# Four conv layers on one core: layer 1's first rows and stack made during layer 0's last filters, the last image's norm on two engines, and the spectral mixing by one matmul per mode

## Chip, cores, metric

The kernel runs on one core of a Trainium2 chip. The metric is the device time of one execution in microseconds (us). Engines are called PE (TensorE), DVE (VectorE), ACT (ScalarE), POOL (GpSimd) and SP (SyncE, which here only issues DMAs). Each engine works through its own instructions in program order and waits on semaphores.

## What is computed

The input x is (8, 32, 128, 128) in f32. Four residual layers follow, each on the group norm of x (32 groups of one channel):

```python
x = x + L0(_gn(x))   # 3x3 conv, batch norm over all images, relu, then a 5x5 and a 3x3 circular filter per channel
x = x + L1(_gn(x))   # n = sqrt(sum_c of 9 shifted squares); op = tanh(n @ op_w.T + op_b), 9x9 for each pixel;
                     # out = W * (patches + patches @ op)
x = x + L2(_gn(x))   # attention from a blurred, Sobel-filtered channel mean
x = x + L3(_gn(x))   # global transform (16 x 16 Fourier modes, top and bottom) times a 3x3 conv
# L3: top = einsum('bixy,ioxy->boxy', c_ft[:, :, :16, :16], w1r + 1j * w1i), bot likewise with w2
```

In L3, each of 32 x 16 kept modes multiplies a complex vector of 32 input channels by its own complex 32 x 32 matrix, for 8 images.

## The kernel before

**Layer 0's filters** (about 300 to 757 us) go image by image (h = 0 to 7), eight turns n of four channels each. A turn is filter5 (L632) and filter3 (L639) on PE, `gradient` on ACT (L957, squares the 3x3 result), `curvature` on DVE (L1423, L1426, and the statistics L1230). Woven into the turns of image h is the finish of image h-1: PE sums its statistics (`group_means`, `group_vars`), DVE makes scale and shift, ACT normalises 32 channels (L938) at turns 1 and 2 and squares them (L964) at 3 and 4, DVE sums the squares over the channels (`channel_sums`, L1435) at 4 and 5, ACT takes the root at 6 (L1021), and DVE splits it into three bf16 parts at 7 (`norm_parts`). With h = 8 the loop runs once more, for the finish of image 7 alone.

SP's part for one finished image, in this order: store x1 (L429), store the normalised image with its borders to `pad1` (L431, "pad"), load a later image, then `shifted_norms`: store the three parts (L369), wait for them to land, and issue 18 copies that lay out shifted rows in `rows_dram` (L376).

**Layer 1** (826 to about 3110 us) has 64 chunks (8 images x 8). A chunk needs the stack (12 DMAs from pad1, `stack_in`, L385), rows of norms (`norms_in`, L393), and operator values that are made once and spread out: `operator_rows` on PE (L661, into PSUM banks 6 and 7 for the first two chunks), tanh on ACT (`rows_tanh_out`, L973), a diagonal added (L979) and a cast (L982) in `rows_high`, a remainder (`rows_rest`, L1458 on DVE for the first two chunks, L1170 on POOL later), `rows_middle` (L987), `rows_low` (L1463 or L1175). Then SP stores them (`split_out`, L399), waits for the landing and issues 24 loads (`split_in`, L410). The tile of the rows is single, so tanh of chunk 1 waits until the store of chunk 0 has landed. The steady work of a chunk is 28 multiplies on DVE (L1498), 14 tanh on ACT (L1041) and 14 multiplies on POOL (L1187), mixed by PE (L703).

Between the layers, with h = 8, SP waits for the rows of image 0 and loads three chunks of norms and the stack; PE makes the operator rows of chunks 0 and 1 between `group_means` and `group_vars` of image 7. ACT's queue holds, in this order: normalise, squares, tanh and rows of both chunks, the root, and then, behind a wait for the landing of image 7's pad store (`xn1_stored[1]`), layer 1's first tanh.

**Layers 2 and 3** go image by image. At the end `mix_spectrum` (L869) mixes the modes: for each of 32 x 16 modes one matmul of 32 x 32 weights with the real part and one with the imaginary part of the weights, 1,024 in all; the f32 matmul stands as two in the trace, so 2,048 records. The four quarters of the partitions (rows of the array) write four different banks at any time. ACT copies the result (L1131), SP stores it and loads it back transposed. PE then makes the last image's conv (`conv3`, L591), ACT takes it out (L1082), and the output loop of 8 images begins (ACT L1139 and L1144, PE L889 and L900, DVE L1584 and L1586), fed by loads of x3 (L504) and l3 (L311).

## Time and profile before

| what | us |
|---|---|
| median of 3 runs | 3891.71 (3881.45 to 3893.06) |
| profiled execution, its own time | 3892.53 |
| its span, first to last instruction | 3890.4 |
| busy PE, DVE, POOL, ACT | 3348.1, 2864.0, 2340.5, 1848.2 |
| last turn of layer 0's filters ends | 757 |
| first multiply of layer 1 on POOL | 826.4 |
| image 7 normalised on ACT | 782.6 to 795.0 |
| mixing of modes | 3609.7 to 3688.3 |

In the page, a row has the start, the length in us, the engine, the line, the operation, the tiles and the count. Many f32 tiles have one name, `arena`, so operations are told apart by their line. A matmul's record is longer than the interval to the next one, since they overlap.

### The profile page before, as it was taken

The numbers are of one execution on the slowest core, as the hardware profiler recorded it, in microseconds if no ns is written. First come the engines' busy times: TensorE is split into PE (matmuls) and PEld (weight loads), VectorE is DVE, ScalarE is ACT, GpSimd is POOL, SyncE is SP. The second block draws the span as 40 slices with busy tenths as digits, with TensorE's granted clock in tenths as the row PEclk, the third lists the DMA queues.
The fourth block names the chain that finished last, engine by engine and source line by source line (L and its number), as shares of the span: only waits on it lengthen the run. The fifth ranks groups of instructions, "written<-read, shape, count | busy, mean of one in ns | idle before, by whom it ended". The sixth has DMA issues, their size and how long they took to land.

```text
span 3890.4 us, 89862 instructions
## 1 busy us (share of the span) xinstructions
PE 3348.1 (86%) x32900; PEld 1193.3 (31%) x32900; DVE 2864.0 (74%) x3513; ACT 1848.2 (48%) x2702; POOL 2340.5 (60%) x1131
## 2 busy tenths in 40 slices
PE   4678999749999999999999999999999957888575
PEld 2343444302212222222222212222222236655454
DVE  3652554459989989989989989989999966666034
ACT  0114566355555555555545545545555546666011
POOL 0000000039999999999999999999999952231000
PEclk9899999969999999999999999999999977889565
DMA  6565897576666656656656656656666654645589
GB/s 158 121 160 108 157 197 169 118 176 151 146 141 154 147 137 154 149 135 154 153 132 159 150 130 159 151 129 157 153 145 145 151 149 123 173 122 132 141 193 253
DMA packets 495205, 586.47 MB, mean 151 GB/s; under 512 B 71971, under 2 KB 334755, under 8 KB 489436
## 3 DMA queue, kind: packets, MB, share of 16 engines
q1 hardware_dynamic: 484212, 563.65, 62.7%
q10 hardware_dynamic: 10560, 16.93, 1.8%
q8 instruction: 287, 4.70, 0.5%
q14 instruction: 146, 1.19, 0.1%
HBM read 409.91 MB, written 184.54 MB: 153 GB/s over the span
## 4 chain that ended last, share of the span: by engine, by line
POOL 30%; PE 29%; issue 28%; DVE 5%; ACT 4%; DMA 2%; SPq 1%; ACTq 0%; POOLq 0%; DVEq 0%
POOL arena L1187 27%; PE ps L632 7%; PE ps L591 7%; PE ps L639 4%; PE ps L703 3%; ACT arena L938 2%; PE ps L789 2%; POOL arena L1175 2%; PE ps L685 1%; DVE arena L1546 1%; PE ps L900 1%; PE ps L869 1%; DMA arena<-x_dram 1%; DMA w_conv<-in_conv_w 1%; DVE arena L1584 1%
## 5 line engine op out<-in xcount | busy, mean ns | idle before, releaser
L1187 POOL TENSOR_TENSOR arena<-arena 128x1024 f32<-128x1024 f32 x896 | 1931.1, 2196 | 555.8 <-ACT arena L1041 555.6
L1498 DVE TENSOR_TENSOR arena<-ps,arena 128x1024 f32<-128x1024 f32 x1792 | 2107.0, 1219 | 206.2 <-PE ps L685 173.9
L703 PE MATMUL ps<-arena,w_mix 128*32 128x512 f32 x10752 | 1439.1, 607 | 79.2 <-POOL arena L1187 79.2
L1041 ACT ACTIVATE arena<-ps 128x1024 f32<-128x1024 f32 x896 | 918.1, 1025 | 1028.2 <-PE ps L695 1017.1
L685 PE MATMUL ps<-arena,sel 48*128 48x512 bf16 x3584 | 703.1, 386 | 25.2 <-issue 15.3
L685 PEld LDWEIGHTS ps<-arena,sel 48*128 48x128 bf16 x3584 | 190.2, 93 | 946.3 <-issue 937.9
L591 PE MATMUL ps<-arena,w_conv 32*32 32x512 f32 x9216 | 357.7, 658 | 46.6 <-issue 38.5
L695 PE MATMUL ps<-norms,opw 57*128 57x512 bf16 x1792 | 348.7, 385 | 49.0 <-ACT arena L973 17.5
L703 PEld LDWEIGHTS ps<-arena,w_mix 128*32 128x32 f32 x10752 | 215.0, 108 | 467.6 <-issue 467.6
L938 ACT ACTIVATE arena<-arena,nmr,rstd 128x128 f32<-128x128 f32 x768 | 299.7, 482 | 31.9 <-DVE nmr L1257 31.9
L632 PE MATMUL ps<-arena,circ 128*128 128x512 f32 x640 | 287.9, 595 | 14.3 <-ACT arena L952 14.3
L591 PEld LDWEIGHTS ps<-arena,w_conv 32*32 32x32 f32 x9216 | 182.5, 108 | 186.4 <-issue 129.1
L695 PEld LDWEIGHTS ps<-norms,opw 57*128 57x128 bf16 x1792 | 101.7, 93 | 435.0 <-issue 429.5
L1219 POOL COPY arena<-arena 32x130 f32<-32x130 f32 x32 | 29.2, 913 | 293.9 <-DVE arena L1548 292.9
L1170 POOL TENSOR_TENSOR arena<-arena 128x1024 f32<-128x1024 f32 x62 | 132.9, 2144 | 96.6 <-ACT arena L982 96.6
L1584 DVE TENSOR_TENSOR arena<-arena,ps 128x512 f32<-128x512 f32 x64 | 43.6, 682 | 195.2 <-PE ps L900 166.3
L639 PE MATMUL ps<-arena,circ 128*128 128x512 f32 x384 | 176.3, 594 | 0.0
L632 PEld LDWEIGHTS ps<-arena,circ 128*128 128x128 f32 x640 | 120.4, 189 | 166.8 <-issue 166.8
L1230 DVE BATCH_NORM_STATS2 st<-arena 128x6 f32<-128x128 f32 x768 | 156.5, 276 | 7.0 <-POOL arena L1206 4.9
L1163 POOL TENSOR_TENSOR col<-col,powers 128x1 f32<-128x1 f32 x8 | 4.4, 550 | 244.0 <-DVE col L1286 244.0
L1426 DVE TENSOR_TENSOR arena<-arena 128x512 f32<-128x512 f32 x64 | 44.3, 692 | 143.1 <-ACT arena L957 141.1
L1175 POOL TENSOR_TENSOR arena<-arena 128x1024 bf16<-128x1024 f32 x62 | 133.0, 2145 | 0.0
(151 smaller groups left out, 2165.2 us busy)
## 6 DMA issues: line engine op xcount, KB each, us to landing
arena<-pad SPq DMA_DIRECT2D x768, 260.0 KB, 7.6
split_dram<-arena SPq DMA_DIRECT2D x64, 768.0 KB, 3.6
arena<-split_dram SPq DMA_DIRECT2D x1536, 32.0 KB, 3.1
x_dram<-arena SPq DMA_DIRECT2D x16, 2048.0 KB, 7.4
l_dram<-arena SPq DMA_DIRECT2D x128, 256.0 KB, 4.3
arena<-l_dram SPq DMA_DIRECT2D x32, 1024.0 KB, 14.0
arena<-x_dram SPq DMA_DIRECT2D x16, 2048.0 KB, 15.8
pad<-arena SPq DMA_DIRECT2D x8, 2080.0 KB, 16.2
```

The lines of the kernel that those rows point to most:

```text
L591: m = pe.matmul(ps[C * j:C * j + C, bank + g, :], weights[C * g:C * g + C, dy, dx, :], tile[C * g:C * g + C, r:r + CR, dx:dx + W], start=t ...
L632: m = pe.matmul(ps[:, n % 2, :], circ[:, d, :], yp[h % 2][:, 4 * n:4 * n + 4, 4 - d:4 - d + W], start=d == 0, stop=d == 4)
L639: m = pe.matmul(ps[:, 2 + n % 2, :], circ[:, 5 + d, :], yp[h % 2][:, 4 * n:4 * n + 4, 4 - d:4 - d + W], start=d == 0, stop=d == 2)
L685: m = pe.matmul(ps[:, 2 * (n % 2) + e, :], sel[ROWS2 * e:ROWS2 * e + SPLIT_ROWS, u % GROUP, :], split[ROWS2 * e:ROWS2 * e + SPLIT_ROWS, pa ...
L695: m = pe.matmul(ps[:, POOL_BANK + e, :], opw[ROWS2 * e:ROWS2 * e + KROWS, SPREAD[c], :], norms[ROWS2 * e:ROWS2 * e + KROWS, buf, half, :]. ...
L703: m = pe.matmul(ps[C * g:C * g + C, SUM + chunk % 2, :], w_mix[:, s, :], ring[:, (first + g // 2) % size, NPX * (g % 2):NPX * (g % 2) + NP ...
L938: m = nc.scalar.activation(tile[:, c, :], src[:, c, :], ACT.Identity, scale=rstd[:, gn.slot + n % 2, c:c + 1], bias=nmr[:, gn.slot + n % 2 ...
L1041: nc.scalar.activation(ring_p[:, slot, :], ps[:, POOL_BANK:POOL_BANK + 2, :].rearrange("p a n -> p (a n)"), ACT.Tanh).then_inc(tanh_p, 1)
L1175: nc.gpsimd.tensor_tensor(hml[:, 2, :], rest, hml[:, 1, :], ALU.subtract).then_inc(rows_l, 1)
L1187: nc.gpsimd.tensor_tensor(slot, slot, pixels(chunk % 2, SPREAD[n // 2], n % 2), ALU.mult).then_inc(prod_p, 1)
L1230: m = nc.vector.bn_stats(st[:, c, :], tile[:, c, :])
L1498: nc.vector.tensor_tensor(slot, weights, pixels(par, ONCE[n // 2], n % 2), ALU.mult).then_inc(prod_d, 1)
```

## The change

It has three parts.

- **Transition.** PE makes the operator rows of chunks 0 and 1 at turns 2 and 5 of image 7's filters, ACT and DVE do their share at turns 3 to 7 (the last cast of chunk 1 at turn 0 behind it). SP loads the norms of chunks 0 to 2 already at image 2. It issues `split_out`, 24 `split_in` and the first stack in the turn of image 7, ahead of `shifted_norms` of image 6. `group_vars` of image 7 follows directly on `group_means`.
- **Last image's norm.** ACT normalises channels 0 to 15 and DVE 16 to 31 (`half_norm`). The squares go by 32 columns of all channels, so that each of DVE's channel sums needs one of them only.
- **Mixing.** The weights of a mode lie as 64 columns (real, imaginary), and one matmul makes both products: 512 matmuls in four groups. Rows 0 to 31 and 32 to 63 now write one bank, rows 64 to 95 and 96 to 127 another. Each group is then put together by four ACT copies (the imaginary products, to the own partitions) and eight DVE operations. The mixing uses all eight banks: it waits for the conv before it to be taken out, and the last conv waits for the putting together. The negated copy of the spectrum (one of three L1075) is gone.

Left out of the diff are semaphore names and counts (`dftw_copy` in threes becomes twos; layer 0's batch-norm uses gn0's semaphores in place of two of its own, with the same waits).

```diff
@@ -187,7 +187,8 @@
...
         dog = sb("dog", [P, W + 2])
-        cs = sb("cs", [P, 3, 2, 4, MODES, B])
+        cs = sb("cs", [P, 2, 2, 4, MODES, B])
+        crossed = sb("crossed", [P, 2, NPX])
         ps = ctx.enter_context(nc.psum_tensor("ps", [P, 8, NPX], F32))
@@ -229,7 +230,7 @@
...
-        wm = part(8192, 4 * C * 64).rearrange("p (r t o m) -> p r t o m", r=2, t=2, o=C)
+        wm = part(8192, 4 * C * 64).rearrange("p (t k m) -> p t k m", t=2, k=2 * C)
         ys = part(37512, 2048).rearrange("p (a b m) -> p a b m", a=8, b=B)
@@ -413,15 +415,6 @@
...
                     rows_in(yt[h % 2], image(y_dram, h + 2), yt_loaded[h % 2])
-                if h == B:
-                    sp.wait_ge(c3_mm, 8 * (B - 1))
-                    sp.wait_ge(xn1_stored[0], 16 * (B // 2))
-                    sp.wait_ge(border_done, 16 * BORDERS)
-                    sp.wait_ge(rows_stored[0], 16 * 18 * (B // 2))
-                    norms_in(0, 0)
-                    stack_in(0, 0)
-                    norms_in(0, 1)
-                    norms_in(0, 2)
                 if h == 0:
@@ -432,10 +425,19 @@
...
                     rows_in(xt[par], image(x, h + 1), xt_loaded[par])
-                if h == B:
+                if h == 2:
+                    sp.wait_ge(rows_stored[0], 16 * 18)
+                    for chunk in range(3):
+                        norms_in(0, chunk)
+                if h == B - 1:
                     split_out(0)
...
                     split_in(0, 1)
+                    sp.wait_ge(c3_mm, 8 * (B - 1))
+                    sp.wait_ge(norm_sq, 4 * (B - 1))
+                    sp.wait_ge(xn1_stored[0], 16 * (B // 2))
+                    sp.wait_ge(border_done, 16 * BORDERS)
+                    stack_in(0, 0)
                 shifted_norms(h - 1)
@@ -463,7 +465,8 @@
...
                     if n + 3 == CHUNKS:
-                        sp.wait_ge(rows_stored[1], 16 * 18 * (B // 2))
+                        for par in range(2):
+                            sp.wait_ge(rows_stored[par], 16 * 18 * (B // 2))
                     norms_in((n + 3) // CHUNKS, (n + 3) % CHUNKS)
@@ -538,8 +541,8 @@
...
-            sp.wait_ge(spec_copy, 8)
             for t in range(2):
+                sp.wait_ge(spec_copy, 2 * t + 2)
                 for q in range(4):
@@ -639,14 +642,6 @@
...
-            for h in range(B):
-                for n in range(8):
-                    filter5(h, n)
-                    if n == 1 and h:
-                        group_vars(gn1, h - 1)
-                    filter3(h, n)
-                    if n == 0 and h:
-                        group_means(gn1, h - 1)
             def chunk_after(b, chunk, n):
@@ -663,13 +658,23 @@
...
+            for h in range(B):
+                for n in range(8):
+                    filter5(h, n)
+                    if n == 1 and h:
+                        group_vars(gn1, h - 1)
+                    filter3(h, n)
+                    if n == 0 and h:
+                        group_means(gn1, h - 1)
+                    if n == 2 and h == B - 1:
+                        pe.wait_ge(op_copied, 32)
+                        pe.wait_ge(par_loaded, 16 * PARS)
+                        operator_rows(0, 0, SUM)
+                    if n == 5 and h == B - 1:
+                        pe.wait_ge(rows_tanh, START + 1)
+                        operator_rows(0, 1, SUM)
             group_means(gn1, B - 1)
-            pe.wait_ge(op_copied, 32)
-            pe.wait_ge(par_loaded, 16 * PARS)
-            operator_rows(0, 0, SUM)
             group_vars(gn1, B - 1)
-            pe.wait_ge(rows_tanh, START + 1)
-            operator_rows(0, 1, SUM)
             pe.wait_ge(gn1.shifted, B)
@@ -859,20 +864,21 @@
...
-                for turn in range(4):
+                for grp in range(4):
                     for m_ in range(KX):
+                        x8, ky = 2 * grp + m_ // MODES, m_ % MODES
+                        t, xx = divmod(x8, 4)
                         for q in range(4):
-                            grp = (turn + q) % 4
-                            x8, ky = 2 * grp + m_ // MODES, m_ % MODES
-                            t, xx = divmod(x8, 4)
-                            for r in range(2):
-                                m = pe.matmul(ps[C * q:C * q + C, 4 + grp, 16 * m_:16 * m_ + 16], wm[C * q:C * q + C, r, t, :, xx * MODES + ky],
-                                              cs[C * q:C * q + C, 1 - r:3 - r, t, xx, ky, :], start=r == 0, stop=r == 1)
-                m.then_inc(spec_mm, 1)
+                            rows, at = slice(C * q, C * q + C), 2 * C * (q % 2)
+                            m = pe.matmul(ps[at:at + 2 * C, 4 * (q // 2) + grp, 16 * m_:16 * m_ + 16], wm[rows, t, :, xx * MODES + ky],
+                                          cs[rows, :, t, xx, ky, :], start=True, stop=True)
+                    m.then_inc(spec_mm, 1)
             pe.wait_ge(wm_loaded, 16 * 16)
-            pe.wait_ge(dftw_copy, 3 * B)
+            pe.wait_ge(dftw_copy, 2 * B)
+            pe.wait_ge(conv3_evac, 2 * (B - 1))
             mix_spectrum()
+            pe.wait_ge(spec_copy, 4)
             for half in range(HALVES):
@@ -963,6 +969,14 @@
...
+            def squares_by_columns(h, q):
+
+                if q == 0:
+                    act.wait_ge(norm_sum, 4 * h)
+                    act.wait_ge(gn1.out, 4 * (h + 1))
+                cols = slice(QC * 4 * q, QC * 4 * q + QC * 4)
+                nc.scalar.activation(sqr[:, :, cols], xn1[h % 2][:, :, 1 + cols.start:1 + cols.stop], ACT.Square).then_inc(norm_sq, 1)
+
             def rows_tanh_out(b, chunk, bank):
@@ -1001,19 +1015,23 @@
...
                         for q in (2 * n - 2, 2 * n - 1):
-                            normalise(gn1, h - 1, q, xn1[(h - 1) % 2][:, :, 1:W + 1], xt[(h - 1) % 2])
+                            if h < B or q < 2:
+                                normalise(gn1, h - 1, q, xn1[(h - 1) % 2][:, :, 1:W + 1], xt[(h - 1) % 2])
                     if n in (3, 4) and h:
                         for q in (2 * n - 6, 2 * n - 5):
-                            squares(h - 1, q)
-                    if n == 3 and h == B:
-                        act.wait_ge(c3_mm, 8 * B)
+                            if h < B:
+                                squares(h - 1, q)
+                            else:
+                                squares_by_columns(h - 1, q)
+                    if n == 3 and h == B - 1:
                         rows_tanh_out(0, 0, SUM)
                         rows_high(0, 0)
-                    if n == 4 and h == B:
+                    if n == 4 and h == B - 1:
                         rows_middle(0, 0)
+                    if n == 6 and h == B - 1:
                         rows_tanh_out(0, 1, SUM)
                         rows_high(0, 1)
-                    if n == 5 and h == B:
+                    if n == 7 and h == B - 1:
                         rows_middle(0, 1)
@@ -1071,9 +1089,9 @@
...
                 sp_ = ps[:, 4, 256:256 + 8 * 2 * MODES].rearrange("p (x r y) -> p r x y", x=8, r=2)
-                for n, (r, sign) in enumerate(((1, -1.0), (0, 1.0), (1, 1.0))):
-                    nc.scalar.activation(cs[:, n, :, :, :, t:t + 1].rearrange("p t x y b -> p (t x) (y b)"),
-                                         sp_[:, r, :, :], ACT.Copy, scale=sign).then_inc(dftw_copy, 1)
+                for r in range(2):
+                    nc.scalar.activation(cs[:, r, :, :, :, t:t + 1].rearrange("p t x y b -> p (t x) (y b)"),
+                                         sp_[:, r, :, :], ACT.Copy).then_inc(dftw_copy, 1)
@@ -1125,15 +1143,16 @@
...
-            act.wait_ge(spec_mm, 1)
-            for n in range(8):
-                src = ps[:, 4 + n // 2, 256 * (n % 2):256 * (n % 2) + 256].rearrange("p (y r b) -> p b r y", y=MODES, r=2)
-                nc.scalar.copy(ys[:, n, :, :].rearrange("p b (r y) -> p b r y", r=2), src).then_inc(spec_copy, 1)
-
+            for grp in range(4):
+                act.wait_ge(spec_mm, grp + 1)
+                after(act, spec_copy, grp - 1)
+                for q in range(4):
+                    at = 2 * C * (q % 2) + C
+                    m = nc.scalar.copy(crossed[C * q:C * q + C, grp % 2, :], ps[at:at + C, 4 * (q // 2) + grp, :])
+                m.then_inc(spec_cross, 1)
             for half in range(HALVES):
...
             act.wait_ge(spec_loaded, 16)
-            act.wait_ge(spec_copy, 8)
             with act.Fori(0, B) as b:
@@ -1429,9 +1448,19 @@
...
+            def half_norm(h):
+
+                dve.wait_ge(gn1.ready, h + 1)
+                dve.wait_ge(xn1_stored[h % 2], 16 * (h // 2))
+                for q in (2, 3):
+                    for c in range(QC * q, QC * q + QC):
+                        m = nc.vector.tensor_scalar(xn1[h % 2][:, c, 1:W + 1], xt[h % 2][:, c, :], rstd[:, gn1.slot + h % 2, c:c + 1],
+                                                    nmr[:, gn1.slot + h % 2, c:c + 1], ALU.mult, ALU.add)
+                    m.then_inc(gn1.out, 1)
+
             def channel_sums(h, q):
-                dve.wait_ge(norm_sq, 4 * h + 4)
+                dve.wait_ge(norm_sq, 4 * h + (4 if h < B - 1 else q + 1))
                 nc.vector.tensor_reduce(r2[:, 32 * q:32 * q + 32], sqr[:, :, 32 * q:32 * q + 32].rearrange("p c w -> p w c"),
@@ -1469,17 +1498,20 @@
...
                         group_scale(gn1, h - 1, t)
+                        if h == B:
+                            half_norm(B - 1)
                     if h < B:
...
                             channel_sums(h - 1, q)
-                    if n == 4 and h == B:
+                    if n == 4 and h == B - 1:
                         rows_rest(0, 0)
-                    if n == 5 and h == B:
+                    if n == 5 and h == B - 1:
                         rows_low(0, 0)
-                    if n == 6 and h == B:
+                    if n == 7 and h == B - 1:
                         rows_rest(0, 1)
+                    if n == 0 and h == B:
                         rows_low(0, 1)
@@ -1569,6 +1601,17 @@
...
                     group_scale(gn2, i + 2, t)
+
+            for grp in range(4):
+                dve.wait_ge(spec_cross, grp + 1)
+                for q in range(4):
+                    at = 2 * C * (q % 2)
+                    real, imag = (tile.rearrange("p (x y r b) -> p r x b y", x=2, r=2, b=B)
+                                  for tile in (ps[at:at + C, 4 * (q // 2) + grp, :], crossed[C * q:C * q + C, grp % 2, :]))
+                    own = ys[C * q:C * q + C, 2 * grp:2 * grp + 2, :, :]
+                    nc.vector.tensor_tensor(own[:, :, :, 0:MODES], real[:, 0], imag[:, 1], ALU.subtract)
+                    m = nc.vector.tensor_tensor(own[:, :, :, MODES:KX], real[:, 1], imag[:, 0], ALU.add)
+                m.then_inc(spec_copy, 1)
```

## Rows read from the trace of the kernel before

**Rows 1.** Windows: us, busy per engine (x), clock, DMA share, GB/s.

```profile
1150.00:3250.00 2100.00, 1938.96 (x14797) 464.07 (x14796) 1884.07 (x1734) 1097.59 (x1238) 1928.67 (x902) 0.98 0.63 146
```

**Rows 2.** Timeline of SP's DMA issues between layer 0 and layer 1.

```profile
761.19 11.36 SPq L376 DMA_DIRECT2D rows_dram<-parts_dram  x18
...
776.14 5.89 SPq L385 DMA_DIRECT2D arena<-pad  x12
...
785.22 0.47 SPq L429 DMA_DIRECT2D x_dram<-arena  x1
794.99 0.38 SPq L431 DMA_DIRECT2D pad<-arena  x1
813.05 0.36 SPq L399 DMA_DIRECT2D split_dram<-arena  x1
816.53 11.06 SPq L410 DMA_DIRECT2D arena<-split_dram  x24
...
827.63 0.42 SPq L369 DMA_DIRECT2D parts_dram<-rp  x1
```

**Rows 3.** Timeline of the other engines there; in brackets the idle time before.

```profile
779.32 1.04 PE L661 MATMUL ps<-norms,opu 57*32 57x512 bf16 x8 [20.94 <-DMA norms<-rows_dram]
...
798.16 1.02 ACT L973 ACTIVATE arena<-ps 128x1024 f32<-128x1024 f32 x1
...
807.11 1.22 DVE L1458 TENSOR_TENSOR arena<-arena 128x1024 f32<-128x1024 f32 x1
...
825.33 1.02 ACT L1041 ACTIVATE arena<-ps 128x1024 f32<-128x1024 f32 x1
826.43 8.58 POOL L1187 TENSOR_TENSOR arena<-arena 128x1024 f32<-128x1024 f32 x4 [528.18 <-ACT arena L1041]
...
871.67 3.49 DVE L1498 TENSOR_TENSOR arena<-ps,arena 128x1024 f32<-128x1024 f32 x3 [4.62 <-DMA arena<-pad]
```

**Rows 4.** Timeline of DVE and ACT in image 7's filters.

```profile
743.83 3.68 DVE L1435 TENSOR_REDUCE r<-arena 128x32 f32<-128x1024 f32 x2
...
755.46 0.60 ACT L957 ACTIVATE arena<-ps 128x512 f32<-128x512 f32 x1 [6.09 <-PE ps L639]
```

**Rows 5.** The chain that ended last, in order of time.

```profile
781.58 12.01 DMA arena<-pad
```

**Rows 6.** Line L429 (x1 store), and the landing times of its DMAs.

```profile
L429 SPq DMA_DIRECT2D x_dram<-arena x8: 468/4720/5405, 370.5 to 785.2; - x8
...
DMA to landing us min/median/max: 6.8/15.0/15.6
```

**Rows 7.** DMA issues, 740 to 850 us: size, us to landing.

```profile
pad<-arena SPq DMA_DIRECT2D x1, 2080.0 KB, 15.8
```

**Rows 8.** Windows: one in the gap between the layers.

```profile
775.00:785.00 10.00, 2.03 (x12) 1.09 (x12) 0.74 (x3) 2.68 (x8) 0.00 (x0) 0.50 0.87 186
```

**Rows 9.** Timeline of the mixing of modes and what follows.

```profile
3610.67 2.12 ACT L1082 ACTIVATE arena<-ps,bias 128x1024 f32<-128x1024 f32 x2 [9.24 <-PE ps L591]
3613.37 2.05 PE L869 MATMUL ps<-cs,arena 32*32 32x16 f32 x128 [1.70 <-issue]
...
3621.50 2.05 PE L869 MATMUL ps<-cs,arena 32*32 32x16 f32 x128 [6.08 <-issue]
...
3688.15 11.65 PE L591 MATMUL ps<-arena,w_conv 32*32 32x512 f32 x280
3688.38 2.31 ACT L1131 COPY arena<-ps 128x256 f32<-128x256 f32 x8 [75.59 <-PE ps L869]
...
3723.56 3.50 PE L900 MATMUL ps<-k,arena 64*128 64x128 f32 x32
...
3727.20 0.69 DVE L1584 TENSOR_TENSOR arena<-arena,ps 128x512 f32<-128x512 f32 x1 [127.34 <-PE ps L900]
```

**Rows 10.** Line L869 in the mixing: ns min/median/max of a record.

```profile
L869 PE MATMUL ps<-cs,arena x2048: 173/212/236, 3609.7 to 3688.1; 32*32 32x16 f32 x187
```

**Rows 11.** Windows: one in the mixing.

```profile
3660.00:3680.00 20.00, 10.66 (x667) 10.12 (x670) 0.00 (x0) 0.00 (x0) 0.00 (x0) 0.50 0.02 4
```

19 lines of the change are left out of this document (10 added, 9 removed).

## Prediction

> **What bounds the kernel now.** I read the windows by stage first. In layer 1, POOL is busy 1929 of 2100 us and DVE 1884 [rows 1]. Nothing in the change shortens a steady chunk, so this stage keeps its length. What can move is the way into it and the way out of the mixing.
>
> Then I read the gap between the last filter turn (757) and POOL's first multiply (826.4), in the timelines [rows 2, 3]. PE's operator rows wait 20.9 us for norms, and image 7's variances stand behind them in PE's queue. Normalise, squares, tanh, the split and the root follow each other on ACT, and layer 1's first tanh comes at 825.3. Image 7's pad store, which that tanh also needs, was issued at 795.0 and landed 15.8 us later, at 810.8 [rows 2, 7]: it is the next thing late once ACT's queue is empty.
>
> Last, the mixing. PE executes 128 records in 2.05 us and then stands still, 6.1 us when the DMA engines are busy [rows 9]. With them idle (share 0.02) it still does only 667 records in 20 us, one block of 128 in 3.8 us [rows 11]. The wait is called issue: nothing in the program holds PE. It looks like the supply of instructions, in blocks of 128 record pairs. So the count of records sets the time. Behind the mixing come the last conv and the output loop, in series.
>
> **Transition.** The filters stay paced by PE, which gains two times eight operator matmuls, 1.04 us at the low clock [rows 3], about 0.7 each at the full one. ACT and DVE have room but take turns. DVE's turn 5 ends its channel sums at 747.5 [rows 4]. Ahead of that now come the 0.7 us of PE, one operation of 1.2 us (as at 807.1 [rows 3]) and a wait of about 1.2 us for ACT, which has to cast first. Behind it comes another 1.2 us. So the split of chunk 0 is ready at about 752.
>
> ACT in turn 6 waits for its store to land and then makes chunk 1. The last gradient, at 755.5 before [rows 4], slips to about 760.5, and DVE adds a subtraction and the last `rows_low`. Scale and shift of image 7 are ready at about 769, 13 us earlier than before, and all 32 channels by 775, since each engine takes 16. The sums of squares and the root end at 784 to 786. All this has stopped mattering, because of SP.
>
> SP's queue is now the path. Each step by its row:
> - split of chunk 0 stored at 752, landed 3.5 us later as at 813.05 [rows 2]: 755.4
> - 24 `split_in` issues, 11.1: 766.5
> - 12 stack issues, 5.9: 772.4
> - store of image 6's parts, queued behind the stack's 3 MB. The stack took from 776.14 to 793.6 before [rows 2, 5], 17.5 us, so about 784. That a store waits for what was issued before it is how I read the x1 store, 6.8 us alone and 15.0 at the median [rows 6].
> - 18 row copies, 11.4: 795.4
> - x1 and pad stores, issued at once after. x1 takes 6.8, plus 1 for the last rows: 803.2. The pad landed 10.0 us after x1 before (810.8 against 785.2 + 15.6): 813.2.
> - ACT's table change and first tanh, then POOL, some 2.4 us: first multiply at 815.6.
>
> That is 10.8 us earlier than 826.4. A little more comes in chunk 1, where DVE waited 4.6 us for the stack at 871.7 [rows 3]. From the landing of image 7's parts (830) to that point went 41.6 us of SP work. Now the parts land with the pad at about 813, so the stack is there at 855, and it is wanted 40.6 us after POOL's start, at 856. I take 3.5 us of gain. **Transition: 14 us.**
>
> Bounds: if the parts do not wait for the stack, they land at 775, the rows are issued by 786, the pad lands at 804 and the gain is about 23. If split or pad come some 5 us later each, it is 2. I stay by the first, since the x1 row is the nearest to it.
>
> The norm loads at image 2 cost SP six issues in a pause that it spends waiting for the norm's parts, so nothing. One L1075 of three less and the renamed semaphores change no wait that lasts: nothing.
>
> **Mixing.** Removed are 1,024 of 2,048 records. The start waits for ACT to take out the conv, until 3612.8 [rows 9]. Before, the mixing's first records lay among the conv's last ones and flowed alone from 3610.4, so this is 2.4 us later. The blocks then follow at PE's old pace: 8.1 us each while loads run, 3.8 after. The first 78 records, seven blocks and a rest bring 1,024 to about 3659.5, against 3688.3. Behind the last group come four ACT copies and eight DVE operations. The copies are as the eight of half the size at 3688.38, 2.3 us [rows 9]. For DVE the bounds are 0.35 us, half of a 512-element one, and the whole 0.69 [rows 9]; an operation of 256 elements has some fixed part, so I take 0.41, 3.3 us in all, and 0.4 for the two hand-overs. The last conv starts at 3665.5 in place of 3688.15. The store and load of the spectrum, moved by the same amount, still hide under the conv's 25 us. **Mixing: 22 us**, and the output loop moves up whole: its first tiles are loaded long before, as the idle DMA engines show [rows 11].
>
> Unknown is a record with 64 columns. The nearest rows are 16 ns for 32 columns now (2.05 us over 128) and 109 ns for 128 columns (L900, 3.50 us over 32 [rows 9]). Up to 29 ns the block's 3.8 us hide it. At half of 109, 55 ns, two late blocks and a rest grow by some 7 us: gain 15. With the long DVE bound it is 20, with the short one 22.5.
>
> The Trainium skill says otherwise on two points. Runtime: NRT & Kernel Launch, section Instruction fetch mechanics, has the fetch of the next block mostly hidden by the issue of the current one. The trace does not agree, with its idle of 1.7 to 6.1 us after a block; by that rule the mixing would save only its records' 16.4 us less 8.4, so 8, and the sum would be 22. TensorEngine Tiling (Array Packing), section Gotcha 1: PSUM Pressure, says that different row tiles cannot access one PSUM bank at the same time, and this change pairs them so. By it the sum would be a loss, the third rival below.
>
> **Sum.** 14 + 22 = 36 us off the profiled execution's 3892.5 gives 3856.5. It stands 0.8 above the median, so I say 3856.
>
> **Rivals.**
> - *Stores slip past the stack.* Gain 23 + 22, 3847 to 3848. For it: SP issues were never seen waiting on a full queue here. Against: the x1 row. 12%.
> - *The mixing is bound by issue.* If the idle is not tied to the count of records, only their own time goes, 1,024 x 16 ns = 16.4 less the 8.4 of the longer start and end (2.4 + 2.3 + 3.3 + 0.4), so 8 remain: 3870. Against it are the even 3.8 us of an idle stretch. 10%.
> - *Two row groups in one bank take turns* (slower). A record then costs its full length of 212 ns [rows 10]: 1,024 make 217 us where 78.6 went, and the kernel takes 3892.5 + 138.4 + 8.4 − 14 = 4025. It decides from 82 ns per record, where the 84 us of saving (14 + 78.6 − 8.4) are used up. Against it: the eight operator matmuls alternate two row groups in one bank, and at 1.2 GHz (0.50 in [rows 8]) 512 columns take 427 ns, eight in turn 3.4 us, yet they took 1.04 [rows 3]. 4%.
> - *The change moves work and no end.* SP's longer queue puts the pad at 822 or later, and the output loop gives back the start by its DMA load (the loop's loads are no faster). Then 3885 to 3892. 7%.
> - *Front as little as 2 us, mixing as forecast.* 3868. 12%.
>
> **Numbers.** The forecast within 8 us has 55%. The range 3838 to 3878 takes in the first, second and last rival and leaves out the slow one and most of the fourth. A measurement tells about 0.3%, 12 us, from no change: faster by over that 0.90, within it 0.05, slower 0.05.
>
> **What would show it.** Right: PE's `group_vars` right behind `group_means`; ACT's first L1041 waiting on the landing of pad, at 813 to 815; 18 L376 of image 6 issued from about 784; L869 with 1,024 records over about 47 us, idle after each 128; the last conv (L591) beginning at 3652, 36 us before 3688.15. Wrong: a first L1041 held by ACT's own work, parts that land within 3 us behind the stack, PE idle without a pattern of 128, or records of L869 further apart than 30 ns.

## The result, and the profile after

The changed kernel takes **3848.68 us** (median of 4 runs, 3843.61 to 3856.77) against 3890.03 for the kernel before in the same comparison (3881.45 to 3893.06): a ratio of 0.9899, with a 95% interval of 0.9875 to 0.9923. The forecast was 3856, in the range 3838 to 3878. The profiled execution took 3846.52 us, 46.0 less than the 3892.5 of the one before.

The head of the page of the changed kernel: busy time of each engine, its share of the span, and its instructions.

```profile
span 3844.3 us, 87849 instructions
PE 3333.0 (87%) x31876; PEld 1180.3 (31%) x31876; DVE 2884.1 (75%) x3561; ACT 1847.0 (48%) x2686; POOL 2340.7 (61%) x1131
```

No engine's share tells anything about a gain at two seams. The steady part of layer 1 is the same work at the same pace, as this window of the changed kernel shows beside [rows 1] (the small differences are its other end, which now reaches 20 us further into the stage behind):

```profile
1150.00:3250.00 2100.00, 1935.37 (x14790) 472.06 (x14790) 1879.01 (x1770) 1094.73 (x1251) 1921.10 (x898) 0.97 0.63 147
```

**Where the time went.** One execution's layer 0 alone differs by several us from the next one's (its first gradient came between 309.9 and 320.6 us in all the runs told of here). So I cut each profile at events that every kernel has, and measure from that first gradient. "Spectrum" is ACT's last copy into `cs`, "loop" the first slice copy of the output loop.

| piece, us | before | after | less |
|---|---|---|---|
| start to first gradient | 316.5 | 313.1 | 3.4 |
| to POOL's first multiply of layer 1 | 509.9 | 497.5 | 12.4 |
| to POOL's last | 2310.7 | 2306.1 | 4.6 |
| to the spectrum | 463.9 | 458.6 | 5.3 |
| spectrum to loop | 114.3 | 96.9 | 17.4 |
| loop to end | 175.1 | 172.1 | 3.0 |

The transition is rows two and three, 17 us; the mixing is the fifth, 17. Together 34 of the 46. Rows one, four and six are not the change's: over all the runs below, whichever parts they hold, the fourth piece lies between 457.7 and 463.9 and the sixth between 170 and 177 (one kernel apart, which is told of).

**The transition.** SP's DMA issues, timeline of the changed kernel (start, us, what, count), against [rows 2]:

```profile
747.94 0.36 SPq L401 DMA_DIRECT2D split_dram<-arena  x1
751.44 11.07 SPq L412 DMA_DIRECT2D arena<-split_dram  x24
762.70 5.83 SPq L387 DMA_DIRECT2D arena<-pad  x12
768.57 0.44 SPq L371 DMA_DIRECT2D parts_dram<-rp  x1
779.93 11.38 SPq L378 DMA_DIRECT2D rows_dram<-parts_dram  x18
791.35 0.58 SPq L422 DMA_DIRECT2D x_dram<-arena  x1
791.98 0.44 SPq L424 DMA_DIRECT2D pad<-arena  x1
792.46 11.06 SPq L371 DMA_DIRECT2D parts_dram<-rp  x1
809.77 11.35 SPq L378 DMA_DIRECT2D rows_dram<-parts_dram  x18
```

Read it downwards: each step begins where the one before ends. The parts of image 6 are issued at 768.57 and their rows cannot follow until 779.93: a store of 97.5 KB takes 11.3 us to land, behind the stack's twelve loads. The last engine to be late is shown by the other timelines (against [rows 3]; in brackets the idle time before, and who ended it):

```profile
739.12 0.61 PE L656 MATMUL ps<-norms,opu 57*32 57x512 bf16 x8
764.55 6.26 ACT L944 ACTIVATE arena<-arena,nmr,rstd 128x128 f32<-128x128 f32 x16 [0.71 <-DVE nmr L1276]
764.49 4.19 DVE L1457 TENSOR_SCALAR arena<-arena,rstd,nmr 128x128 f32<-128x128 f32 x16
779.34 0.31 ACT L1039 ACTIVATE rn<-r 128x128 f32<-128x128 f32 x1 [4.37 <-DVE r L1464]
779.67 1.28 ACT L1059 ACT_TABLE_LOAD   x1
809.47 1.02 ACT L1059 ACTIVATE arena<-ps 128x1024 f32<-128x1024 f32 x1 [28.52 <-DMA pad<-arena]
810.57 8.58 POOL L1206 TENSOR_TENSOR arena<-arena 128x1024 f32<-128x1024 f32 x4 [515.60 <-ACT arena L1059]
841.87 2.15 POOL L1189 TENSOR_TENSOR arena<-arena 128x1024 f32<-128x1024 f32 x1 [3.54 <-ACT arena L996]
877.35 2.15 POOL L1189 TENSOR_TENSOR arena<-arena 128x1024 f32<-128x1024 f32 x1 [1.16 <-ACT arena L996]
```

ACT has finished image 7 by 781 and then stands 28.5 us: the pad store, not the engines, sets the first tanh of layer 1. The pad store took 17.5 us from issue to landing. The last two lines are the same operation of two successive chunks, 35.48 us apart, which is the steady distance; before, the same two stood 39.8 apart, with the 4.6 us wait for the stack in [rows 3].

**The mixing.** Timeline of the changed kernel, against [rows 9]:

```profile
3589.01 2.12 ACT L1100 ACTIVATE arena<-ps,bias 128x1024 f32<-128x1024 f32 x2 [13.25 <-PE ps L594]
3591.28 5.91 PE L873 MATMUL ps<-cs,arena 32*64 32x16 f32 x206 [2.30 <-ACT arena L1100]
3598.71 3.72 PE L873 MATMUL ps<-cs,arena 32*64 32x16 f32 x128 [1.52 <-issue]
3607.39 3.72 PE L873 MATMUL ps<-cs,arena 32*64 32x16 f32 x128 [4.96 <-issue]
3613.32 3.72 PE L873 MATMUL ps<-cs,arena 32*64 32x16 f32 x128 [2.21 <-issue]
3619.26 7.24 PE L873 MATMUL ps<-cs,arena 32*64 32x16 f32 x256 [2.22 <-issue]
3627.03 5.47 PE L873 MATMUL ps<-cs,arena 32*64 32x16 f32 x178 [0.52 <-issue]
3632.53 2.34 ACT L1151 COPY crossed<-ps 32x512 f32<-32x512 f32 x4 [5.65 <-PE ps L873]
3634.91 0.56 DVE L1612 TENSOR_TENSOR arena<-ps,crossed 32x256 f32<-32x256 f32 x1 [3.71 <-ACT crossed L1151]
3639.22 10.00 PE L594 MATMUL ps<-arena,w_conv 32*32 32x512 f32 x205 [6.72 <-DVE arena L1613]
3651.44 4.75 PE L594 MATMUL ps<-arena,w_conv 32*32 32x512 f32 x83 [2.22 <-issue]
```

The 1,024 records take 41 us where 2,048 took 78.4. The waits still come after each 128 records or a multiple, but a block now executes for 3.72 us: 29 ns a record, not 16. That these waits are for instructions is read from one more thing: both pages have a DMA queue of the kind instruction, with 287 packets (4.70 MB) before and 279 (4.57 MB) after. That is 16.4 KB a packet and eight packets fewer for 1,024 records fewer, one for each 128. Behind the mixing PE stands 6.7 us, and then the last conv takes 17.05 us to its first evacuation (3639.22 to 3656.27), where it took 11.7 before (3688.15 to 3699.84). Two windows of the changed kernel, the hand-over and the first 6 us of that conv (us, busy per engine, granted clock, DMA share, GB/s):

```profile
3632.00:3639.00 7.00, 0.49 (x14) 0.39 (x10) 4.05 (x8) 2.31 (x4) 0.00 (x0) 0.50 0.01 2
3639.00:3645.00 6.00, 5.78 (x99) 2.66 (x102) 0.16 (x1) 0.00 (x0) 0.00 (x0) 0.50 0.76 175
```

### The profile page after: what moved, and what is told of

Read it like the earlier page. It is cut to its first block, busy times and chain, and to the rows that moved or that the text cites. A ratio compares the mean times of both kernels' runs of the same rounds, so it can differ in the third digit from the quotient of the medians.

```text
span 3844.3 us, 87849 instructions
## 1 busy us (share of the span) xinstructions
PE 3333.0 (87%) x31876; PEld 1180.3 (31%) x31876; DVE 2884.1 (75%) x3561; ACT 1847.0 (48%) x2686; POOL 2340.7 (61%) x1131
## 3 DMA queue, kind: packets, MB, share of 16 engines
q8 instruction: 279, 4.57, 0.5%
## 4 chain that ended last, share of the span: by engine, by line
POOL 30%; PE 29%; issue 28%; DVE 6%; ACT 4%; DMA 2%; SPq 1%; ACTq 0%; POOLq 0%; DVEq 0%
POOL arena L1206 28%; PE ps L594 7%; PE ps L635 7%; PE ps L642 4%; PE ps L708 3%; ACT arena L944 2%; PE ps L794 2%; POOL arena L1194 2%; PE ps L690 1%; DVE arena L1578 1%; PE ps L906 1%; PE ps L816 1%; DMA arena<-x_dram 1%; DVE arena L1627 1%; PE ps L873 1%
## 5 line engine op out<-in xcount | busy, mean ns | idle before, releaser
L594 PE MATMUL ps<-arena,w_conv 32*32 32x512 f32 x9216 | 356.8, 654 | 54.9 <-issue 39.8
```

The source lines that it names most:

```text
L594: m = pe.matmul(ps[C * j:C * j + C, bank + g, :], weights[C * g:C * g + C, dy, dx, :], tile[C * g:C * g + C, r:r + CR, dx:dx + W], start=t ...
```

## The experiments

Each ratio is to the kernel before, run in the same comparison, with its 95% interval. Edits are to the changed kernel unless said otherwise.

**1 and 2. Each half alone.** The first has the new transition and the old mixing, the second the new mixing and the old transition (both as the diff of the change has them, the other functions left as they were).

> The changed kernel with the old mixing (1,024 matmuls of 32 columns). If the parts of the change add up as the changed kernel's trace has them, this keeps the transition's 20 us (POOL's first multiply near 810.6, no wait for the stack in chunk 1) and loses the rest: 20 to 22 us faster than the kernel before, 3868 to 3871. If the 5 us that the changed kernel also gained between layer 1 and the mixing belong to the new transition, it is 25. If they come with the shorter mixing code or with one L1075 less, 20.

> The kernel before with the new mixing alone. Adding up: 17.7 us from the last L1075 to the output loop and the 3 us in the output loop, so 18 to 21 us faster than before; with the 5 us of the layers between, 23 to 26. POOL's first multiply stays at 826.

Measured: transition alone 3868.99 us, 0.9956 (0.9940 to 0.9972); mixing alone 3866.1, 0.9954 (0.9936 to 0.9972). Of 3883.6 that is 17 and 18 us less, 35 together, against forecast terms of 14 and 22. By stage the first gains 12.2 up to POOL's first multiply and 6.8 up to its last, and has its old 114.0 from spectrum to loop; the second has 97.4 there and its POOL starts at the old 510.4. Each median difference is known to some 6 us either way, so they show independence only roughly; the pieces by stage (12 + 7 and 17 alone, 12 + 5 and 17 together) agree with it, as the sum assumed.

**3. Four row groups in four banks again.** Each of the four row groups works in a bank of its own at any moment; ACT then has to wait for the whole mixing.

```
-                for grp in range(4):
+                for turn in range(4):
...
+                            grp = (turn + q) % 4
...
-                act.wait_ge(spec_mm, grp + 1)
+                act.wait_ge(spec_mm, 4)
```

> The changed kernel with the four row groups writing four different banks at any time (the groups rotated as in the kernel before); the four groups are then put together only after the whole mixing. Theory A (the 29 ns of a record come from loading 64 columns): 128 records still take 3.7 us. Theory B (two row groups in one bank hinder each other): they fall to some 2.1 us, 16 ns per record. In time it loses either way what the three first groups had hidden, 3 x 6.6 us = 20 us at most: 3860 to 3869 by A, some 5 us less by B.

```profile
3605.40 3.72 PE L874 MATMUL ps<-cs,arena 32*64 32x16 f32 x128 [4.41 <-issue]
```

Measured: 3864.89 us, 0.9949 (0.9932 to 0.9966), and the same 3.72 us per 128. So the 29 ns belong to the record with its 64 columns of weights, not to the shared bank. Spectrum to loop took 108.2 us in place of 96.9, since PE stands 19.6 us at the end while ACT and DVE take out all four groups. That places the value of the new order of the groups: three of the four are taken out while PE mixes, and PE's pause is 6.7 us in place of 19.6. The Trainium skill, TensorEngine Tiling (Array Packing), section Gotcha 1: PSUM Pressure, has different row tiles unable to access one bank at the same time; in these two kernels the pairing made no difference that the records show.

**4. Rows of image 6 behind the image store.** `shifted_norms` is cut into the parts' store and the row copies; the image and pad stores go ahead of image 6's row copies.

```
+                if h == B:
+                    rows_out(B - 2)
-                shifted_norms(h - 1)
+                parts_out(h - 1)
+                if h != B - 1:
+                    rows_out(h - 1)
```

> The changed kernel with the 18 row copies of image 6 issued behind the x1 and pad stores of image 7; only its parts store stays where it was. Theory: SP's queue and the order of transfers set the start of layer 1. Then both stores are issued at about 771 in place of 791, the pad lands at 779 (stack) + 7 + 10 = 797, and POOL starts at 798 to 800, 11 to 13 us earlier: 3836 to 3838. Rival: the DMA engines are what is full, and the order changes nothing: the pad lands at 805 or later and the time stays within 3 us of the changed kernel's. Rival two: the split of chunk 1 comes late, and a wait in chunk 1 gives part of it back (a wait for the stack in chunk 1 of some us).

SP's timeline, and the wait that came in chunk 1:

```profile
754.44 0.36 SPq L404 DMA_DIRECT2D split_dram<-arena  x1
850.10 5.85 DVE L1537 TENSOR_TENSOR arena<-ps,arena 128x1024 f32<-128x1024 f32 x5 [3.93 <-DMA arena<-pad]
```

Measured: 3841.55 us, 0.9886 (0.9869 to 0.9902). From the split's store to POOL's first multiply went 50.8 us (754.44 to 805.27) where the change needs 62.6 (747.94 to 810.57), 12 us less. 3.9 us of it came back in chunk 1, where the next stack is now late: from the first gradient to POOL's last multiply it is 2794.9 us where the change has 2803.6. The medians alone, taken in two comparisons, would not tell 0.9886 from 0.9899. That SP's queue is the path of the transition is shown by these pieces, and so is what is late next.

**5. Both sets of row copies in the pauses of the first chunks.** As 4, but image 6's copies follow chunk 1's loads and image 7's follow chunk 2's (chunk 0's were issued before this loop).

```
-                shifted_norms(h - 1)
+                parts_out(h - 1)
+                if h < B - 1:
+                    rows_out(h - 1)
...
+                if n < 2:
+                    rows_out(B - 2 + n)
```

> The kernel with the rows of image 6 put off, gone one step further: the row copies of images 6 and 7 are issued behind chunk 1's and chunk 2's loads. In e4_rows_later the stores moved up as meant, and 4 us came back as a wait for chunk 1's stack, since 36 row copies stood ahead of it in SP's queue. Theory: with them behind it, POOL starts 11 to 12 us earlier than in the changed kernel (50 to 51 us after the split of chunk 0 is stored, not 62.6) and chunk 1 has no wait: 11 to 12 us faster than the changed kernel in all, 16 to 18 us before it some of which the run to run spread of layer 0 hides. Rival: the row copies, wherever they stand, take their transfer time from the loads of a chunk, and chunk 2 or 3 waits 3 us or more.

```profile
795.47 1.02 ACT L1066 ACTIVATE arena<-ps 128x1024 f32<-128x1024 f32 x1 [15.36 <-DMA pad<-arena]
```

Measured: 3837.22 us, 0.9869 (0.9853 to 0.9885). POOL starts at 796.57, and its first three chunks stand 35.5 us apart each, with no wait for the stack. By stage, gradient to POOL's last multiply is 2789.5 where the change has 2803.6: 14 us. Nothing needs those rows early: with 8 chunks of 35.5 us an image, the norms of image 6 are wanted some 1,700 us later.

**6. A mixing without loads beside it.** The output loop's first loads are issued behind the spectrum's instead of before it.

```
-            l3_in(0)
-            l3_in(1)
...
-            x3_in(0)
...
-            x3_in(1)
...
-            x3_in(2)
...
+            l3_in(0)
+            l3_in(1)
...
+            x3_in(0)
...
+            x3_in(1)
...
+            x3_in(2)
```

> The changed kernel with the loads for the output loop (l3 of two images, x3 of three) issued behind the spectrum's load, so that the DMA engines have little to do during the mixing. Theory (PE waits for the supply of its instructions, which competes with the loads): the blocks of 128 records follow every 3.7 to 4 us from the start, and the mixing takes 32 to 35 us in place of 41.4. Rival (the wait after a block is PE's own and fixed): blocks as far apart as in the changed kernel, 5.9 to 8.7 us in the first half. The time is worse as a whole, by the loads that now stand ahead of the output loop, 10 us or more.

```profile
3587.02 5.91 PE L873 MATMUL ps<-cs,arena 32*64 32x16 f32 x206 [2.30 <-ACT arena L1100]
3593.32 23.64 PE L873 MATMUL ps<-cs,arena 32*64 32x16 f32 x818 [0.39 <-issue]
3593.00:3617.00 24.00, 23.57 (x818) 23.11 (x818) 12.67 (x24) 6.93 (x13) 0.00 (x0) 0.50 0.12 27
```

Measured, in one run: 3836.35 us. 818 records follow each other at 28.9 ns without a pause, in a window whose DMA share is 0.12 (in the change's mixing, 0.83), and the mixing takes 29.7 us (first start to last) in place of 40.9 to 46.2. Spectrum to loop is 84.3 us where the change has 96.9. The loss in the output loop that I expected did not come: loop to end is 175.4, within the others' 170 to 177. So the waits called issue, 11 to 16 us of them, come from the loads that run beside them. The Trainium skill, Runtime: NRT & Kernel Launch, section Instruction fetch mechanics, has the fetch of the next block mostly hidden by the issue of the current one. Here that held when the DMA engines were quiet and a block executed for 3.7 us; with the loads beside it it did not, and [rows 9, 11] show it failing for a block of 2.05 us.

**7. Banks by group.** Group `grp` uses banks 2·grp and 2·grp + 1, so the last conv, whose banks are among the first four, needs only the first two groups to be out.

```
-  m = pe.matmul(ps[at:at + 2 * C, 4 * (q // 2) + grp, ...
+  m = pe.matmul(ps[at:at + 2 * C, 2 * grp + q // 2, ...
...
-            pe.wait_ge(spec_copy, 4)
+            pe.wait_ge(spec_copy, 2)
```

> The changed kernel with group g of the mixing in banks 2g and 2g+1 in place of g and 4+g, so that the last conv (banks 0 to 3) needs the first two groups alone. Theory: PE goes from the mixing to the conv without the 6.7 us of idle, and the conv's first half takes 11.7 to 14 us in place of 17.1, because its instructions are there and its cold start is not longer. 8 to 12 us from the mixing's end to the output loop, 3838 to 3841 beside the changed kernel's 3849. Rival: the load of the spectrum, which used to hide under the conv, comes on the path, or the conv waits for instructions as before: a gain of 6.7 us or less.

```profile
3638.64 5.24 PE L873 MATMUL ps<-cs,arena 32*64 32x16 f32 x178 [0.52 <-issue]
3643.81 11.91 PE L594 MATMUL ps<-arena,w_conv 32*32 32x512 f32 x288
3644.00:3650.00 6.00, 6.00 (x130) 2.83 (x118) 3.67 (x7) 2.23 (x4) 0.00 (x0) 0.62 0.01 3
```

Measured: 3837.3 us, 0.9863 (0.9845 to 0.9881). The 6.7 us of idle PE are gone, and the conv's first half takes 11.91 us, as before the change. Spectrum to loop is 87.6 us. From the conv's start to the loop it is 30.6 to 33.8 us in every kernel where PE stands idle before it (the change, experiments 2, 3, 4, 5, 10), against 27.2 to 28.4 without the pause (before, experiments 1, 7, 8, 11). Where the deferred loads lie beside it, it is 35.2 with the pause (6) and 31.5 without (9, 12), where PE stops 4.2 us for instructions after the conv's 461st record.

What the pause costs inside the conv is read beside the kernel before (first line) and experiment 2 (the others):

```profile
3688.00:3694.00 6.00, 6.00 (x151) 3.29 (x147) 0.00 (x0) 2.31 (x8) 0.00 (x0) 0.63 0.39 93
3662.00:3668.00 6.00, 5.99 (x144) 3.10 (x153) 0.00 (x0) 0.00 (x0) 0.00 (x0) 0.72 0.73 175
3662.01 8.92 PE L593 MATMUL ps<-arena,w_conv 32*32 32x512 f32 x205 [6.72 <-DVE arena L1585]
3674.43 4.87 PE L593 MATMUL ps<-arena,w_conv 32*32 32x512 f32 x83 [3.49 <-issue]
```

A low clock at the start is not the main cost (0.50 is the 1.2 GHz level, 1.00 the 2.4 GHz one). Experiment 2 has the pause and ran its first 6 us at 0.72, higher than the 0.63 before, and its first evacuation still came 17.35 us after the conv's start. What all seven kernels with a pause share is a stop after the conv's 205th record, 2.2 to 3.5 us long: the next record starts 12.2 to 12.8 us behind the conv's start, and 7.7 to 8.8 in the seven kernels without a pause, none of which stops there. The instruction queue agrees: in the change no packet of it starts between 3633 and 3648.5 us, and in experiment 7 one does within 5 us of the conv's start. Where the clock falls behind the stop, this adds to it: the last 83 records of the first half take 4.75 us in the change (window 3651 to 3657: 0.72) and 3.29 in experiment 3 (1.00). Whether the pause alone brings the stop, or the spectrum's store and load too, is open: their share of the DMA engines in the conv's first 6 us is 0.76 in the change and 0.01 in experiment 7, but before it was 0.39, then 0.77, with no stop.

**8. Variances first, in the kernel before.** Is the old transition late because PE's operator rows stand ahead of image 7's variances? The edit to the kernel before:

```
+            group_vars(gn1, B - 1)
             pe.wait_ge(op_copied, 32)
             pe.wait_ge(par_loaded, 16 * PARS)
             operator_rows(0, 0, SUM)
-            group_vars(gn1, B - 1)
```

> The kernel before with one statement moved: PE makes image 7's variances ahead of chunk 0's operator rows, not behind them. Theory (what holds the start of layer 1 in the changed kernel is SP's queue and the pad store, not the making of the rows): normalise starts near 762 in place of 782, x1 and pad are issued at 785 behind the stack, the pad lands at 804 to 811, ACT is ready at about the same time, and POOL starts at 809 to 813, which is where the changed kernel has it: 12 to 17 us faster than before, most of the new transition's 20 us. Rival (the early rows are what pays): ACT's queue with both chunks' rows ends at 820 or later, and the gain is under 6 us.

```profile
785.17 1.26 SPq L431 DMA_DIRECT2D pad<-arena  x1
796.02 8.99 SPq L399 DMA_DIRECT2D split_dram<-arena  x1
split_dram<-arena SPq DMA_DIRECT2D x1, 768.0 KB, 15.3
811.38 1.02 ACT L973 ACTIVATE arena<-ps 128x1024 f32<-128x1024 f32 x1 [19.02 <-DMA split_dram<-arena]
```

Measured: 3879.71 us, 0.9980 (0.9968 to 0.9992); 12 to 17 us were expected, and the rival had it. The pad store is 10 us earlier, but the split's store now stands behind it, lands after 15.3 us (3.5 in the kernel before), and ACT's queue brings the first tanh only to 820. Up to POOL's first multiply it gains 3.2 us from the first gradient (506.7 against 509.9). Making the rows early, which the change does, is what takes the split off this path; earlier norms alone do not.

**9. All three edits, 5, 6 and 7.**

> The changed kernel with the three edits of e5_rows_last, e6_quiet_mixing and e7_banks_by_group together. By the stages of those runs: the transition is 14 us shorter than in the changed kernel. The mixing takes 30 us, the conv begins at its end and takes 25.5, so that from the last spectrum copy to the output loop there are some 70 us in place of 97 to 100. In all 36 to 42 us below the changed kernel, 3806 to 3813 us. Rival: with the loads behind the mixing and the conv moved up, the first loads of the output loop land after it could begin, and it gives back 5 to 15 us of this: 3815 to 3825, with a wait of DVE for x3 or l3 in its first image.

Timelines of this kernel, its image loads and the first operation that needs them; below, the same loads in experiment 6:

```profile
3643.76 5.99 SPq L514 DMA_DIRECT2D arena<-x_dram  x3
3659.05 0.69 DVE L1634 TENSOR_TENSOR arena<-arena,ps 128x512 f32<-128x512 f32 x1 [38.36 <-DMA arena<-x_dram]
3724.44 0.69 DVE L1634 TENSOR_TENSOR arena<-arena,ps 128x512 f32<-128x512 f32 x1 [17.06 <-DMA arena<-x_dram]
```

```profile
3646.10 5.89 SPq L507 DMA_DIRECT2D arena<-x_dram  x3
```

Measured: 3831.57 us, 0.9862 (0.9839 to 0.9886), not the 3806 to 3813 expected. Spectrum to loop fell to 74.6, the sum of the gains, but loop to end rose to 183.7. Counted from the last spectrum copy, the loop can begin 9.7 us earlier than in 6 (74.6 against 84.3) and the image loads are no earlier (issued at 73.1, against 71.6): they queue behind the spectrum's stores and the `l3` loads. Most of the 38 us in the first row is the time of the conv, in which DVE has nothing to do; its first operation comes 13.8 us behind the loop's start, where it is 10.7 to 13.3 in the others. The loss is at a later image, 17 us of wait where 6 has 8.6 at most, and 31.0 us for that image where 6 has 22.3. That in 6 the later start of the loop covered the loads is how I read this.

**10. The last image's norm on ACT alone.** `half_norm` and the squares by columns are taken out, and ACT normalises all 32 channels.

```
-                            if h < B or q < 2:
+                            if True:
...
-                        if h == B:
-                            half_norm(B - 1)
```

> The changed kernel with image 7 normalised by ACT alone and its squares by channels, as in the kernel before. Theory (SP's queue and the pad store set the start of layer 1): all channels are normalised 6 us later, at 777, which is still ahead of the pad store's turn at 791, and the root 10 us later, at some 790, well ahead of the pad's landing at 808. Nothing moves: within 3 us of the changed kernel. Rival: the later parts store of image 7 delays chunk 1 by up to 5 us.

```profile
794.14 0.31 ACT L1036 ACTIVATE rn<-r 128x128 f32<-128x128 f32 x1 [7.23 <-DVE r L1461]
816.20 1.02 ACT L1056 ACTIVATE arena<-ps 128x1024 f32<-128x1024 f32 x1 [20.45 <-DMA pad<-arena]
```

Measured: 3849.2 us, 0.9901 (0.9884 to 0.9917), the same as the whole change. The split was stored at 754.07 here, 6.1 us later than in the change's profile, and the first tanh is 6.7 later. The root comes 14.8 us later than in the change, of which those 6.1 are the later start, and ACT still waits 20 us for the pad. The split of the norm over two engines is worth nothing in this kernel.

**11. Edits 5 and 7 together.**

> The edits of e5_rows_last and e7_banks_by_group together, with the loads for the output loop where the changed kernel has them. In e10_all_three the output loop took 183.7 us in place of 172 to 176, waiting 78 us in all for x3, so the quiet mixing gave back about what it gained. By the stages: transition 14 us shorter than in the changed kernel, 87 to 89 us from the last spectrum copy to the output loop in place of 97, the loop 170 to 176. In all 22 to 24 us below the changed kernel, 3824 to 3828, and better than the kernel with all three edits by some 5 us. Rival: the output loop is bound by its transfers whenever it starts, and takes 180 us here too.

Measured: **3819.96 us** (3815.44 to 3836.59), 0.9832 (0.9811 to 0.9853): by the ratios 65 us under the kernel before, where the change is 39 under it. That is 4 to 8 us better than expected; spectrum to loop took 84.0 us, not 87 to 89.

**12. As 11, with the loads of only the first image early.** `l3_in(0)` and `x3_in(0)` stay where they are, the other three go behind the spectrum's load.

> As e8_two_edits, but of the output loop's five early loads only those of the first image (l3 and x3) are issued ahead of the mixing; the other three stand behind the spectrum's load. Theory: 4 MB of loads are over some 15 us after the mixing began, so its last two thirds run without waits, 33 to 36 us in place of 42 to 46, and the first image of the loop does not wait. What the other loads then cost the loop decides: if as in e10_all_three, 8 us, the time is that of e8_two_edits within 4 us; if less than half of it, it is 4 to 8 us better. Rival: slower than e8_two_edits by over 4 us, because the later images wait.

Measured: 3822.18 us, 0.9830 (0.9816 to 0.9843), not to be told from 11. The mixing fell from 43.2 to 34.6 us, spectrum to loop from 84.0 to 78.2, and loop to end stayed at 174.0 (172.4 in 11), with no wait for an image over 8.6 us. Spectrum to end, 252.2 us, is 4 us less than in 11; the medians do not show it, and whether it is real stays open.

## Why the prediction was right

The sum, 36 us, came out as 34 by stage and as 35 by the two halves alone. The medians differ by 41, and by the ratio's interval the gain is 30 to 49 us; experiment 10, which does what the change does but for the norm, came out 37 under the kernel before. So the 7 us between 3856 and 3849 say nothing about a mechanism. The same goes for the first rival, stores that slip past the stack, which had 3847 to 3848: its number came and its mechanism did not. Within the sum the transition was forecast 3 to 5 us too small and the mixing 5 too large, and that these cancelled is luck.

**Transition, forecast 14, measured 17 to 19.** The step that was to become the path, SP's queue, did.
- The split of chunk 0 was stored at 747.9, not 752. Some 3.4 of these 4 us are layer 0's, which was earlier in this execution (316.5 against 313.1).
- `split_in` and stack went as their rows, 11.1 and 5.8.
- The parts of image 6, behind the stack: 11.3 us from issue to landing, at 779.9 (forecast 784, the 4 us carried on). The first rival, stores that slip past, is false in the trace. Its argument that SP was never seen waiting at an issue was misread: in [rows 6] the issue of an x1 store takes SP 4.7 us at the median and 0.5 at the least, and in the change one issue of a parts' store takes 11.06.
- Rows done at 791.3 (795.4). The pad landed 17.5 us after its issue, at 809.5 (17.8 were forecast), and POOL began at 810.6 (815.6). Counted from the first gradient that is 12.4 us of gain against 10.8.
- Chunk 1: 4.3 gained against 3.5. The remaining 0.3 of the 4.6 in the table is spread; the transition alone showed 6.8 there, so the piece is known to some 2 us.
- The root of image 7 was ready at 779.7 (forecast 784 to 786), and it did not matter, as forecast; experiment 10 delays it by 9 us at no cost.

**Mixing, forecast 22, measured 17.** The pieces, counted here from ACT's first copy of the last image's spectrum (0.2 to 0.4 us before the last copy) to the loop, each to the end of its last record:

| us | before | forecast | after | 2 | 5 | 7 | 11 |
|---|---|---|---|---|---|---|---|
| to the first record | 9.1 | 12.3 | 16.2 | 13.2 | 12.9 | 13.5 | 12.4 |
| records | 78.6 | 46.7 | 41.2 | 44.8 | 45.6 | 46.5 | 43.5 |
| PE idle behind them | 0 | 6.0 | 6.7 | 6.7 | 6.7 | 0 | 0 |
| conv to loop | 27.2 | 27.2 | 32.9 | 32.8 | 33.4 | 27.9 | 28.4 |

- Start and records together: 59.0 forecast, 57.4 measured, 58.0 to 60.0 in experiments 2, 5 and 7, 55.9 in 11. The count of records is what sets the time, blocks of 128 with waits between, at the pace forecast, as long as the loads run beside it (experiment 6, without them: 29.7 us). In the change's profile the conv ahead of the mixing had a wait of 2.6 us for instructions, so its records began later; that they therefore ran with less disturbance by the loads is not shown. The rival "bound by issue", 3870, is false.
- A record of 64 columns, the unknown: 29 ns, the very edge up to which the block's supply was said to hide it. It did: PE's executing time grew and its waiting shrank. Nothing in the prediction said where between 16 and 109 ns the record would lie, so this edge was met by luck.
- DVE's "3.3 us in all": eight operations of 0.56 us, starting 0.53 apart, made 4.3. This is the whole of the difference between 6.0 and 6.7 and a little more.
- **The step that failed** is the last conv, "starts at 3665.5 in place of 3688.15" and lasts the same 25 us, costed as a piece that moves without changing. It got 5.7 us longer. The wait that it left out is PE's own, for instructions behind the pause: 2.2 us after the 205th record, where the conv before had none. The rest is slower execution, 10.00 + 4.75 us against 11.65, so 3.1 us: about 1.0 of it before the stop, at a clock of 0.50 where the conv before had 0.63 in its first 6 us, and about 1.5 behind it, where the clock was low again (what is left of the 3.1 is the length of the 205th record itself, which stands alone there). Experiment 7 removes the pause, and all of it goes: 11.91 us for the half. Experiment 2 shows that the stop comes without the low clock at the start.

**The slow rival**, row groups taking turns in one bank (4%), is false: 29 ns per record, not 212, and the same with four banks (experiment 3). **"Moves work and no end"** did not happen either: the output loop is 172.1 us, and the pad landed at 809.5. The range left out the first of these and most of the second; its width was for the first, second and last rival, and none of them came.

## What to carry to other kernels

When engines get room, look at the queue that issues the DMAs: a small store that something waits for takes the place in line of everything issued before it, so what is wanted late (here 36 row copies wanted some 1,600 us later) goes behind what is wanted next. A piece that is "moved whole" need not be moved whole if an idle stretch of PE comes ahead of it; look for the buffers whose assignment creates the pause, which here cost one index to mend. And two gains that were each measured alone need not add up: deferring loads was free while the loop behind was late, and made it 11 us longer (183.7 against 172) once it was not.

## What the runs showed of the hardware

- A small store behind large transfers in one queue: 97.5 KB landed in 2.1 to 2.6 us in the kernel before, in 11.3 behind the stack's twelve loads, and in 17.3 behind the 2 MB image and pad stores. 768 KB took 3.5 us alone and 15.3 behind the pad store. SP itself was held at the issue too, 11.06 us at one store in the timeline above.
- PE's instruction supply and the DMA loads share something: 29 ns records ran without waits at a DMA share of 0.12, and stood 0.5 to 5.0 us between blocks of 128 at about 0.8. Both at the same granted clock of 0.50.
- A conv behind a pause of PE of 6.7 or 19.6 us stopped after 205 records for 2.2 to 3.5 us, in all seven kernels with such a pause, at a clock of 0.50 to 0.72 in its first 6 us; without a pause none did.
- A float32 record of 16 columns with 32 x 64 weights took 29 ns at a granted clock of 0.50, and 16 ns with 32 x 32 weights. The number of banks in use made no difference.
- A root of the whole tile and the following table change on ACT cost 0.31 and 1.28 us, and the table change came ahead of the wait for the pad, so it cost the path nothing.
